# Turning the next step's input and keys with VectorE blocks and 32 DMAs instead of TensorE transposes

## The reference, cut to what matters

```python
h = layernorm(x) * (1 + ca) + sa
x = x + ga * attention(h)
h = layernorm(x) * (1 + cb) + sb
x = x + gb * ffn(h)
```

```python
v  = h @ Ww.T
rk = h / norm(h) per head ; wk = rk moved on by one token
A  = inv(I + strict(wk wk^T * L)) ; intra = strict(rk wk^T * L)
v_new = A v - (A wk) S
o  = (rk * gp) S + intra v_new
S  = gamma^C S + (wk * gp_tail)^T v_new
out = h + (o * alpha) @ Wr.T
```

```python
h = silu(w1 x * s1) * (w2 x * s2)
h = gelu(h1 h * s) ; h = gelu(h2 h * s) ; y = w3 h * s3
```

## Time and profile before

| | us |
|---|---|
| median of 3 runs | 1740.12 (1738.30 to 1741.58) |
| profiled execution, own time | 1740.26 |
| its span in the trace | 1738.4 |

### The profile page before, as it was taken

The page is one execution under the profiler, slowest core; times in us unless marked ns, Lnnn a source line. Parts: engine busy times, 40 slices in busy tenths (PEclk is TensorE's granted clock), DMA queues, the critical chain, the costliest instruction groups (busy, mean ns, idle before and its releaser), DMA issues.

```text
span 1738.4 us, 60948 instructions
## 1 busy us (share of the span) xinstructions
PE 1710.8 (98%) x25488; PEld 1645.9 (95%) x25488; DVE 1100.7 (63%) x3137; ACT 965.3 (56%) x2249; POOL 593.5 (34%) x694
## 2 busy tenths in 40 slices
PE   8799999999999999999999999999999999999999
PEld 5699999999999999999999999999999999999998
DVE  5677666666666666666666666666666666666432
ACT  4664555555555555555555555555555555555554
POOL 3544333243333243333243333243333243333111
PEclk8899999999999999999999999999999999999999
DMA  8201000000000000000000000000000000000000
GB/s 273 87 17 30 12 23 23 18 21 14 22 23 24 17 21 11 24 23 24 18 20 13 22 23 23 17 21 14 21 23 23 17 21 17 18 23 17 6 4 14
DMA packets 37360, 47.12 MB, mean 27 GB/s; under 512 B 9236, under 2 KB 29336, under 8 KB 37080
## 3 DMA queue, kind: packets, MB, share of 16 engines
q1 hardware_dynamic: 35088, 40.75, 8.5%
q10 hardware_dynamic: 1992, 2.38, 0.5%
HBM read 22.53 MB, written 8.39 MB: 18 GB/s over the span
## 4 chain that ended last, share of the span: by engine, by line
PE 93%; ACT 1%; DVE 1%; POOL 1%; issue 1%; DVEq 0%; ACTq 0%
PE mlp L1153 64%; PE mlp L1225 6%; PE solo L1153 3%; PE duo L1421 3%; PE solo L1294 3%; PE solo L1126 2%; PE duo L1342 1%; PE duo L1119 1%; PE duo L1410 1%; PE duo L1315 1%; PE duo L1114 1%; PE solo L1430 1%; PE solo L1136 1%; PE duo L1412 1%; PE duo L1306 1%; PE duo L1277 1%
## 5 line engine op out<-in xcount | busy, mean ns | idle before, releaser
L1153 PE MATMUL mlp<-act_hi,w_hi 128*128 128x256 f32 x4096 | 968.9, 283 | 1.1 <-POOL act_lo L654 0.6
L1153 PE MATMUL mlp<-act_lo,w_hi 128*128 128x256 f32 x4096 | 946.3, 277 | 0.2 <-issue 0.2
L1153 PEld LDWEIGHTS mlp<-act_hi,w_hi 128*128 128x128 f32 x4096 | 769.8, 188 | 10.1 <-POOL act_lo L654 1.4
L1153 PEld LDWEIGHTS mlp<-act_lo,w_hi 128*128 128x128 f32 x4096 | 770.2, 188 | 1.3 <-issue 0.4
L791 ACT ACTIVATE full<-mlp,scale_sb 128x256 f32<-128x256 f32 x512 | 246.7, 482 | 554.2 <-PE mlp L1153 554.0
L881 DVE TENSOR_TENSOR act_lo<-full,act_hi 128x256 fp32r<-128x256 f32 x512 | 240.6, 470 | 339.2 <-ACT act_hi L792 336.3
L654 POOL TENSOR_TENSOR act_lo<-full,act_hi 128x256 fp32r<-128x256 f32 x256 | 186.8, 735 | 493.4 <-ACT act_hi L781 493.4
L792 ACT ACTIVATE act_hi<-mlp,scale_sb 128x256 fp32r<-128x256 f32 x512 | 243.9, 476 | 0.0
L1153 PE MATMUL mlp<-xh,w_hi 128*128 128x256 f32 x768 | 185.7, 282 | 4.3 <-issue 3.4
L1153 PE MATMUL mlp<-xl,w_hi 128*128 128x256 f32 x768 | 184.9, 281 | 0.0
L593 POOL TENSOR_TENSOR rstd<-ve,minus_half 128x2 f32<-128x2 f32 x64 | 48.7, 761 | 335.4 <-DVE ve L830 335.0
(11 more groups left out here) (178 smaller groups left out, 2660.9 us busy)
## 6 DMA issues: line engine op xcount, KB each, us to landing
w_raw<-in_wts SPq DMA_DIRECT2D x22, 512.0 KB, 5.4
kg<-r SPq DMA_DIRECT2D x64, 126.0 KB
xin<-in_x SPq DMA_DIRECT2D x62, 128.0 KB
out_y<-y SPq DMA_DIRECT2D x62, 128.0 KB, 2.5
step_and_inv<-square_t SPq DMA_DIRECT2D x56, 64.0 KB, 2.0
wmod_sb<-in_wmod ACTq DMA_DIRECT2D x1, 1024.0 KB, 9.6
kg<-last SPq DMA_DIRECT2D x64, 2.0 KB
last<-r SPq DMA_DIRECT2D x64, 2.0 KB, 1.7
```

The lines of the kernel that those rows point to most:

```text
L1153: mm = pe.matmul(dst, *general_ops, start=is_first and i == 0, stop=is_last and i == 1)
```

## The change

Two VectorE items, flip 0 and flip 1, take the place of start in the mixed steps. flip 0 turns each 32x32 block of h (chunk n+2) within itself, from SBUF to SBUF, into h_blocks, which is the memory of near. flip 1 does the same for r into r_blocks, the memory of cross, and makes the small copy of the last column. 16 DMAs then carry the blocks of h to their places in hT, and 16 the blocks of r to theirs in rT; each moves 32 partitions x 4 pieces of 128 bytes. SP issues all 32 (move_blocks) behind its store of the result. values waits on TensorE for both sets of DMAs. hT's layout changes to (batch, half, token), with the transposes and the copy of the earlier steps changed to match.

The list changes with it: norm2 stands ahead of l3's column 0; fs, expand and so on stand one column earlier; stats stands before lead; flip 0 behind norm at l2's column 0; unit before state at l2's column 4, and flip 1 behind state; residual of the next chunk moves from l2's column 6 to l3's column 2 of the next step. On SP the loads and the keys of the step keep their place; they wait for residual. Columns 0 and 1 of l3 are woven together on TensorE: the last of eight input tiles of column 0 comes after three of column 1.

```diff
+BETWEEN = 3
+SQ = 32
+SQS = P // SQ
+MOVES = 16 * SQS * SQS
...
-    hT = sb("hT", [KT, NB, P])
+    hT = sb("hT", [NB, KT, P])
...
+    h_blocks, r_blocks = (t[:].rearrange("p e q n -> p (e q n)") for t in (near, cross))
...
-    mixed = listed([("rg", 0, 0), ("start", 0, 1)], late + layers[:2 * HK], {
-        ("l3", 0): [("norm2", 0, 0)],
-        ("l3", 1): [("values", 0, 1), ("pred", 0, 0), ("gram", 0, 1), ("turn", 0, 0), ("intra", 0, 1), ("u", 0, 0)],
-        ("l3", 2): [("fs", 0, 1)],
-        ("l3", 3): [("fs", 1, 1)],
-        ("l3", 4): [("fs", 2, 1)],
-        ("l3", 5): [("ln2", 0, 0), ("fs", 3, 1)],
-        ("l3", 6): [("ln2", 1, 0), ("expand", 0, 1)],
+    mixed = listed([("rg", 0, 0), ("norm2", 0, 0)], late + layers[:2 * HK], {
+        ("l3", 1): [("values", 0, 1), ("pred", 0, 0), ("gram", 0, 1), ("turn", 0, 0), ("intra", 0, 1), ("u", 0, 0), ("fs", 0, 1)],
+        ("l3", 2): [("fs", 1, 1), ("residual", 0, 1)],
+        ("l3", 3): [("fs", 2, 1)],
+        ("l3", 4): [("fs", 3, 1)],
+        ("l3", 5): [("ln2", 0, 0), ("expand", 0, 1)],
+        ("l3", 6): [("ln2", 1, 0)],
         ("l3", 7): [("parts", 0, 0), ("silu", 0, 0), ("y", 0, 0), ("y", 1, 0)],
-        ("l1", 7): [("lead", 0, 0), ("far", 0, 1), ("stats", 0, 2)],
-        ("l2", 0): [("old", 0, 0), ("norm", 0, 2)],
+        ("l1", 7): [("stats", 0, 2), ("lead", 0, 0), ("far", 0, 1)],
+        ("l2", 0): [("old", 0, 0), ("norm", 0, 2), ("flip", 0, 2)],
         ("l2", 1): [("keys", 0, 0)],
         ("l2", 2): [("join", 0, 0), ("square", 0, 2)],
         ("l2", 3): [("length", 0, 2)],
-        ("l2", 4): [("n", 3, 1), ("state", 0, 0)],
-        ("l2", 5): [("unit", 0, 2)],
-        ("l2", 6): [("attn_out", 0, 0), ("residual", 0, 2)],
+        ("l2", 4): [("n", 3, 1), ("unit", 0, 2), ("state", 0, 0), ("flip", 1, 2)],
+        ("l2", 6): [("attn_out", 0, 0)],
...
+            def move_blocks(a, p):
+                sp.wait_ge(v_full, a)
+                sp.wait_ge(h_turned, a - 3)
+                blocks_of = h_blocks.rearrange("p (q c n) -> p q c n", q=NP, n=SQ)
+                for i in range(SQS):
+                    for c in range(SQS):
+                        to = hT[SQ * c:SQ * c + SQ].rearrange("p b k n -> p (b k) n")
+                        sp.dma_start(to[:, :, SQ * i:SQ * i + SQ], blocks_of[SQ * i:SQ * i + SQ, :, c, :]).then_inc(hT_in, 16)
+                sp.wait_ge(pred_full, a - 2)
+                sp.wait_ge(rg_ready, a - 2)
+                sp.wait_ge(r_turned, a - 3)
+                blocks_of = r_blocks.rearrange("p (q c n) -> p q c n", q=NP, n=SQ)
+                for i in range(SQS):
+                    at = 1 + SQ * (i % 2)
+                    for c in range(SQS):
+                        sp.dma_start(rT[p][SQ * c:SQ * c + SQ, :, i // 2, at:at + SQ], blocks_of[SQ * i:SQ * i + SQ, :, c, :]).then_inc(rT_in, 16)
...
+                if items in (third, mixed) and (whole or n + 2 < STEPS):
+                    move_blocks(n + 2, g)
...
+                    if name == "flip" and k == 0:
+                        dve.wait_ge(h_ready, now)
+                        dve.transpose(h_blocks, h[:].rearrange("p b d -> p (b d)")).then_inc(h_turned, 1)
+                    if name == "flip" and k == 1:
+                        dve.wait_ge(r_ready, now)
+                        dve.transpose(r_blocks, r[:].rearrange("p b d -> p (b d)")).then_inc(r_turned, 1)
+                        rT_cols, before = (rT[i][:].rearrange("p q c n -> p (q c) n") for i in (p, 1 - p))
+                        dve.tensor_copy(rT_cols[:, :, 0:1], before[:, :, C:C + 1]).then_inc(rT_ready, 1)
...
+                    paired = name == "l3" and k < 2 and items is mixed and not general
+                    if paired and k == 0:
+                        layer("l3", 0, range(HK - 1))
+                    if paired and k == 1:
+                        layer("l3", 1, range(BETWEEN))
+                        layer("l3", 0, range(HK - 1, HK))
+                        layer("l3", 1, range(BETWEEN, HK))
...
                         if items is mixed:
-                            pe.wait_ge(rT_ready, n + 1)
+                            pe.wait_ge(hT_in, MOVES * n - 2 * MOVES)
+                            pe.wait_ge(rT_in, MOVES * n - 2 * MOVES)
+                            pe.wait_ge(diag_ready, n + 1)
+                            pe.wait_ge(rT_ready, now)
                             pe.wait_ge(prod_ready, nth(n - 1, HK - 3))
+                            pe.wait_ge(ao_scaled, n)
+                            pe.wait_ge(state_ready, n)
```

More of the change, by code:

```diff
@@ L338, in main @@
         ("l2", 1): [("solve", 1, 0), ("fs", 3, 1), ("expand", 0, 1), ("stats", 0, 2)],
-        ("l2", 2): [("state", 0, 0), ("norm", 0, 2)],
+        ("l2", 2): [("state", 0, 0), ("norm", 0, 2), ("flip", 0, 2)],
         ("l2", 3): [("far", 0, 1), ("n", 1, 1), ("square", 0, 2)],
-        ("l2", 4): [("length", 0, 2), ("attn_out", 0, 0), ("residual", 0, 2)],
-        ("l2", 5): [("n", 2, 1), ("unit", 0, 2)],
+        ("l2", 4): [("length", 0, 2), ("attn_out", 0, 0)],
+        ("l2", 5): [("n", 2, 1), ("unit", 0, 2), ("flip", 1, 2)],
         ("l2", 7): [("n", 3, 1)],
@@ L400, in tokens, with moved @@
         return dram[c::2, rows, :].rearrange("b p d -> p b d")
+    def moved(a):
+        return not isinstance(a, int) or a > 3
     def second_one(a):
@@ L534, in step @@
                 whole = not isinstance(n, int)
-                if items is mixed and (whole or n + 1 < STEPS):
-                    attention(n + 1, 1 - g)
                 if whole or 2 <= n <= STEPS + 1:
@@ L540, in step @@
                         load_last(n - 1)
+                    if items is mixed and (whole or n + 1 < STEPS):
+                        attention(n + 1, 1 - g)
                     if items is third:
@@ L738, in part @@
                         act.wait_ge(hT_full, now)
-                        act.copy(hT[:].rearrange("p k b n -> p (k b n)"), turned_h(a)).then_inc(hT_ready, 1)
+                        act.copy(hT[:].rearrange("p b k n -> p (b k n)"), turned_h(a)).then_inc(hT_ready, 1)
                     if name == "values":
@@ L1154, in product, with layer @@
                     return mm
-                def layer(name, k):
+                def layer(name, k, js=range(HK)):
                     bank = gated[k % 3] if name == "l1" else mlp[k % 2]
@@ L1182, in layer @@
                         w = (BLK_H1 if i == 1 else BLK_H2) + HK * k
[L1183 to L1199, removed]
+                        if js[0] == 0:
+                            if k < 2:
+                                pe.wait_ge(prod_ready if i == 1 else l_act[i - 1], nth(m, HK - 2 + k))
+                            if k >= 2:
+                                pe.wait_ge(l_act[i], nth(m, k - 2))
+                            if general:
+                                weights_in(m, unit[name, k])
+                            if items is mixed and name == "l2" and k == 2 and (not isinstance(n, int) or n + 1 < STEPS):
+                                pe.wait_ge(inv_moved, 32 * n - 64)
+                            if items is second:
+                                pe.wait_ge(rounded[0], k + 1)
+                            if i == 2 and isinstance(n, int) and n == 2:
+                                if k < 5:
+                                    pe.wait_ge(rounded[0], 9 + k)
+                                else:
+                                    pe.wait_ge(rounded[1], k)
+                        for j in js:
                             if k == 0:
@@ L1232, in part @@
                     now = a + 1
-                    if name in ("l1", "l2", "l3"):
+                    paired = name == "l3" and k < 2 and items is mixed and not general
+                    if name in ("l1", "l2", "l3") and not paired:
                         layer(name, k)
+                    if paired and k == 0:
[4 more added lines that the diff above has]
+                        layer("l3", 1, range(BETWEEN, HK))
                     if name == "y" and general:
@@ L1276, in part @@
                             for b in range(NB):
-                                mm = pe.transpose(in_h[:, (kt * NB + b) * P:(kt * NB + b + 1) * P], h_a[:, b, kt * P:(kt + 1) * P], ident)
+                                mm = pe.transpose(in_h[:, (b * KT + kt) * P:(b * KT + kt + 1) * P], h_a[:, b, kt * P:(kt + 1) * P], ident)
                         mm.then_inc(hT_full, 1)
@@ L1285, in part @@
                             pe.wait_ge(tables_ready, 1)
-                        pe.wait_ge(hT_ready, now)
+                        if items is not mixed:
+                            pe.wait_ge(hT_ready, now)
                         if items in (second, third):
@@ L1309, in part @@
                         pe.wait_ge(const_in, 16)
-                        pe.wait_ge(hT_ready, now if items is alone else begun(n, items))
-                        pe.wait_ge(rT_ready, now if items is alone else begun(n, items))
```

(6 more changed lines are left out.)

6 lines of the change are left out of this document (4 added, 2 removed).

## The result

| | before | after |
|---|---|---|
| median | 1739.21 us (4 runs) | 1985.66 us (4 runs, 1981.91 to 1990.57) |
| profiled execution, span | 1740.26, 1738.4 us | 1986.90, 1985.1 us |

The changed kernel is slower: ratio 1.1419, 95% interval 1.1388 to 1.145. The sign is the one forecast, the size isn't: 1841 us was forecast, with 1911 us as the upper end.

What follows compares the result with a forecast made beforehand. TensorE bounds the kernel; 32 DMAs issued in one row would stretch its period from 51.74 to 33.2 + 31 x 0.65 + 2.0 = 55.35 us. Over 28 steps that adds 101 us: 1841 us, range 1714 to 1911.

Steps and rivals of the forecast that it cites:

- TensorE is the bound, and its 0.88 us come off: TensorE, 98% busy: dropping eight transposes saves 0.88 us per step, 24.6 us in all, if all else is hidden.
- The l2/l3 boundary needs nothing: TensorE from l2 to l3: act_lo of column 7 comes in time without the transposes, 0.95 us to spare when woven.
- VectorE's part: Two 128x512 block transposes at 0.70 us each replace a 0.68 us copy; no cost on the path as such.
- The DMAs in one row decide: SP's queue before values: 32 DMAs issued one after the other set the period at 55.35 us, 3.6 more than before.
- all 32 in a row: Period term for the whole chain of moves on SP: 33.2 + 31 x 0.65 + 2.0 = 55.35 us.
- values to first h issue: From values until the h moves begin, after norm and flip 0 on VectorE: 33.2 us.
- 31 spacings: SP's issues of the 32 moves, 0.65 us from one to the next: 31 x 0.65 us.
- last issue to next values: From the last move's issue to its landing, for which values waits: 2.0 us.
- Since stats and norm come a fixed stretch of TensorE work after values: The wait before values therefore comes again in every step and can't be worked off: 28 times, 101 us in sum.
- The rule weighed: Skill's rule that starting a DMA is usually small beside the DMA itself; by it all 32 issues would hide.
- Cheap issues: Rival: SP issues the moves at spacings below 0.51 us, all is hidden, 1716 us at 0.45 us; 33%.
- The DMA engines as the bound: Rival: 128-byte packets at 100 ns make the DMA engines the limit, period 64 us, time 2084 us; 4%.

Runs made afterwards that it cites:

- experiment 6: The changed kernel with only h by block transpose and 16 DMAs; r is turned by TensorE again, without flip 1 and the r moves: 1729.98 us, ratio 0.9957.
- experiment 2: The changed kernel without its 32 DMAs; values waits for the two VectorE block transposes alone, output not the reference's: 1724.80 us, ratio 0.992.
- experiment 7: The kernel with only h by block transpose and DMAs, with l3's columns 0 and 1 in plain order, not woven: 1728.97 us, ratio 0.9943.
- experiment 3: The changed kernel with 8 + 8 DMAs of twice the bytes instead of 16 + 16, output not the reference's: 1730.93 us, ratio 0.9959.
- experiment 4: The changed kernel with 12 + 12 DMAs, the four diagonal blocks not moved, output not the reference's: 1794.08 us, ratio 1.0314.
- Experiment 1: The changed kernel with seven extra 128x512 matmuls on TensorE ahead of its waits for the moved blocks, results overwritten: 1940.04 us, ratio to before 1.1166.
- experiment 5: The changed kernel with SP's loop 2 steps long instead of 12, all other engines as they were: 1987.64 us, ratio 1.1426.

## Why the prediction was right in kind and wrong in size

*TensorE is the bound, and its 0.88 us come off.* Right. The 0.44 us of h alone gave 0.42 (experiment 6). Without any moves the two together gave 0.47 of 0.88; the rest went into the wider spacing (experiment 2), which no row of before had shown in l3's columns 2 to 7 or y.

*The l2/l3 boundary needs nothing.* Right for what was run (experiment 7).

*VectorE's part.* Right in size: 0.70 forecast for each flip, 0.71 and 0.70 measured. flip 1 ends 44.4 us after values, not 42.0 (42.5 in the run without moves), but the r moves stand behind the h moves in the queue and don't wait for it.

*The DMAs in one row decide.* Right: with 32, 24 and 16 of them the mean wait before values is 7.07, 1.79 and, with the last 16 wide ones, 0.1 us (experiments 3, 4). The sum was the right one, with three terms. The terms of "all 32 in a row", forecast and measured as means after:

| term | forecast | measured | off |
|---|---|---|---|
| values to first h issue | 33.2 | 36.2 | +3.0 |
| 31 spacings | 20.15 (0.65) | 22.2 (0.716) | +2.1 |
| last issue to next values | 2.0 | 2.2 | +0.2 |
| period | 55.35 | 60.64 | +5.3 |

28 x 5.3 = 148 us, on 1841 us: 1989, against 1985.66 measured. So the miss lies in the first two terms; the first alone, 28 x 3.0 = 84 us, leads to 1925 us and out of the range. That the sum closes this well is partly luck: the 51.74 us of one step stood for the mean period of before, 52.07. From the two means the rise is 28 x 8.57 = 240 us of the 246.6 between the profiled executions.

The step that failed is "Since stats and norm come a fixed stretch of TensorE work after values". The work is fixed, its duration isn't. A TensorE that stood still for some 7 us went on at half its clock, and values, pred and gram lie in that stretch. Experiment 1 took this out and moved the first issue by 1.8 of the 3.0 us. Most of the other 1.2 us is there without a stall too: 34.0 to 34.2 us in experiments 6 and 3. The offset was read from one good step. Over all steps of before norm ends 0.3 us later behind values than in it; another 0.16 us is that the row of the chain, 902.40, begins that much behind the start of values' first matmul, from which the means are taken. The last 0.7 us isn't taken apart.

At 98% busy the steady state of before has no wait to fall behind. But the trace shows the price at its start, where TensorE waited up to 2.0 us at a time and the granted clock was 0.50 from 13.2 to 26.9 us. TensorE in order of time, the first values of all:

```profile
24.77 2.96 PE L1294 MATMUL solo<-wv_sb,hT 128*128 128x256 f32 x8
```

By the same measure, from its first start to its last end, values takes 1.89 us later on, and the 707 ns at the end of the earlier trace rows is the first matmul of this one. I forecast a wait of 4.5 us and didn't ask what TensorE does after it. The Trainium skill (TensorE: Matmul & The Clock Gate, HAM oscillation — how this bites in real kernels) tells of a loop that waits for a DMA in each turn and starts each turn at the slow clock, so that the price is paid every time; the trace agrees, with values at 3.75 us in place of 1.73, and slow in all 28 steps.

The spacing's core was right to 0.01: 0.601 and a gap of 0.043 make 0.645. What was missed are the 8% of issues of 0.7 to 1.9 us, which add 0.06 us to the mean; the last 0.01 is the pause between the two sets. Their like stood in the earlier trace rows, 988 ns as the largest of the token loads, and I took the median.

*The rule weighed.* The Trainium skill (DMA: Bandwidth & Descriptors, Issuing engines are not separate DMA queues) says that starting a DMA is usually small beside it. Here it is a third of it, 0.60 of 1.8 us, and as the issues stand in line and the transfers don't, it is nearly all of the 22 us. The measurement decides against using the rule for DMAs of 16 KB in one queue. Whether a second engine that issues half of them would have hidden them wasn't run.

*The rivals.* Cheap issues: fell, none of 896 was under 0.585 us. The DMA engines as the bound: fell, 12 ns per packet. The 57 ns worked out from the earlier trace rows were of packets of 0.92 MB / 1008 = 913 bytes; the 128-byte packets in the trace of before took 12.6 ns each. The read-modify-write price of pieces under 512 bytes, in the specifications of the skill's DMA page (the Trainium skill, DMA: Bandwidth & Descriptors, Specifications), can't have mattered here: whatever the 12.5 ns hold, the engines were 84% idle. A packet of 256 bytes took 17.3 ns (experiment 3), so fewer bytes per ns go in the smaller ones; no run has the same move in pieces of 512 bytes or more, so the rule itself isn't tested.

## What to carry to other kernels

DMAs that one engine issues in a row cost that engine 0.71 to 0.77 us each in the means of these runs, much the same for 16 KB and 32 KB: count them, and set that sum against the time between the moment the data is there and the moment it is wanted. Half of the change (16 moves, 12 us, in a gap of some 17.7 us) pays; the whole of it (32, 22 us) doesn't. Where the sum says that a TensorE which was never idle will wait for some microseconds, add what it loses at the lower clock behind the wait: 1.6 us per step here, behind waits of some 7 us. And take offsets and durations as means with their tails, not from one good step.

## What the runs showed of the hardware that wasn't expected

- The same stream of 128x256 matmuls, at a granted clock of 1.00 and with nothing in between, runs at 113.4 or at 117.8 ns per matmul, for a whole stretch of 16 to 128 of them. In the kernel before the wide spacing is in l1's 64 (20 of 29 steps) and in one to three groups of 16 of l2 in every step, never in l3's columns 2 to 7 and y. In the kernel without moves it is in these 128 (27 of 29), in the h-only kernels never there. It costs up to 0.55 us per step, over half of what was to be won. It isn't the moves: it is there most of all without them. What sets it stays open.
- VectorE's block transposes of 32 partitions ran with their output in each of the other groups of 32 partitions, at 0.31 us for 128 elements each when eight follow one another.
- A 128-byte packet between two places of SBUF took 12.5 ns of a DMA engine's time and one of 256 bytes 17.3, where those of before, of 913 bytes in the mean, took 57.
- Every one of the 70 slow DMA issues of SP (over 0.7 us, median 0.60) overlapped an instruction fetch, and one in ten of the quick ones did (experiment 5).
